# Loading the expert biases one attention unit sooner, into the room of the attention's operands

## The reference

```python
qk = jnp.einsum('bhdq,bhdl->bhql', qh, kh) * scale
sm = jax.nn.softmax(qk, axis=-1)
ret = jnp.einsum('bhql,bhdl->bhdq', sm, vh)
...
scores = xf @ gate_w.T + gate_b + bias
top_scores, top_idx = jax.lax.top_k(scores, TOP_K)
gates = jax.nn.softmax(top_scores, axis=-1)
comb = jnp.sum(jax.nn.one_hot(top_idx, E, dtype=gates.dtype) * gates[..., None], axis=1)
h = jax.nn.silu(jnp.einsum('td,ehd->teh', xf, w1) + b1)
y = jnp.einsum('teh,edh->ted', h, w2) + b2
out = jnp.einsum('ted,te->td', y, comb)
```

## Time and profile before

| what | us |
|---|---|
| median of 3 runs | 792.31 (791.72 to 800.5) |
| profiled execution, span | 789.6 |
| PE busy | 727.5 (92%) |
| DVE busy | 579.8 (73%) |
| ACT busy | 410.9 (52%) |
| POOL busy | 356.2 (45%) |

### The profile page before, as it was taken

The page is one execution under the profiler, slowest core; times in us unless marked ns, Lnnn a source line. Parts: engine busy times, 40 slices in busy tenths (PEclk is TensorE's granted clock), DMA queues, the critical chain, the costliest instruction groups (busy, mean ns, idle before and its releaser), DMA issues.

```text
span 789.6 us, 14359 instructions
## 1 busy us (share of the span) xinstructions
PE 727.5 (92%) x4237; PEld 305.2 (39%) x4265; DVE 579.8 (73%) x1148; ACT 410.9 (52%) x758; POOL 356.2 (45%) x347
## 2 busy tenths in 40 slices
PE   5989999899999999899999989989996889999992
PEld 2444444344444443222223222222233445555551
DVE  5688889795867778688988888998866775555551
ACT  2543445563636465377787767766783732222220
POOL 4665455113020131536657657767564723443332
PEclk9999999999999999899999999999998899999997
DMA  9999770017273678234343334544446677999963
GB/s 311 384 110 238 264 298 0 1 38 274 83 257 137 211 250 293 52 91 110 95 105 92 107 109 130 153 120 123 122 130 177 170 104 122 150 148 131 131 80 51
DMA packets 114326, 117.51 MB, mean 149 GB/s; under 512 B 54856, under 2 KB 78280, under 8 KB 114128
## 3 DMA queue, kind: packets, MB, share of 16 engines
q1 hardware_dynamic: 103152, 94.48, 42.1%
q0 software_dynamic: 10384, 22.02, 16.7%
q10 hardware_dynamic: 720, 0.13, 0.1%
HBM read 43.61 MB, written 59.56 MB: 131 GB/s over the span
## 4 chain that ended last, share of the span: by engine, by line
PE 43%; DVE 7%; issue 3%; SPq 1%; ACT 1%; DMA 1%; DVEq 1%; POOL 0%; POOLq 0%; ACTq 0%
PE l_b L1504 8%; PE l_a L1128 7%; PE l_pv L1515 7%; PE l_sm L1523 7%; PE l_pv L1149 4%; PE l_sm L1149 4%; PE l_a L1449 2%; PE l_b L1462 2%; DVE l_negm L1723 1%; PE l_a L1138 1%; PE l_b L1495 1%; DMA t_room<-in_b 1%; DVE h_negm L1723 1%; SPq L1073 1%; PE l_b L1456 1%
## 5 line engine op out<-in xcount | busy, mean ns | idle before, releaser
L1633 ACT ACTIVATE t_room<-l_b 128x512 f32<-128x512 f32 x256 | 139.1, 594 | 39.7 <-PE l_b L1504 38.9
L1128 PE MATMUL l_a<-w1h,h_stack 128*128 x312 | 78.9, 321 | 5.5 <-DVE l_stack L1181 3.9
L1723 DVE TENSOR_REDUCE l_negm<-l_a 128x2 f32<-128x1024 f32 x64 | 75.2, 1220 | 11.4 <-PE l_a L1449 11.4
L1723 DVE TENSOR_REDUCE h_negm<-l_a 128x2 f32<-128x1024 f32 x56 | 65.9, 1220 | 14.2 <-PE l_a L1449 14.2
L1157 ACT ACTIVATE l_stack<-l_stack 128x352 f32<-128x352 f32 x39 | 19.4, 496 | 106.3 <-DVE l_stack L1181 106.3
L1515 PE MATMUL l_pv<-t_room,l_vt 128*32 128x512 f32 x512 | 70.1, 620 | 0.1
L1523 PE MATMUL l_sm<-t_room,ones_f 128*32 128x512 f32 x512 | 69.5, 615 | 0.0
L825 PE MATMUL ps_st<-f_xt,wg 128*128 128x512 fp8e4 x256 | 65.7, 379 | 0.8 <-ACT f_xt L729 0.8
L825 PE MATMUL ps_r<-f_xt,wg 128*128 128x512 fp8e4 x256 | 65.7, 379 | 0.0
L974 POOL TENSOR_TENSOR X<-X,f_y 128x512 f32<-128x512 f32 x16 | 20.0, 1249 | 79.9 <-ACT f_y L875 79.9
L1128 PE MATMUL l_a<-w1l,h_stack 128*128 x156 | 50.2, 322 | 0.0
(11 more groups left out here) (301 smaller groups left out, 1572.6 us busy)
## 6 DMA issues: line engine op xcount, KB each, us to landing
slots_x<-empty SPq DMA_DIRECT2D x8, 2376.0 KB, 11.2
slots_x<-empty SPq DMA_DIRECT2D x7, 2112.0 KB, 16.3
h_stack<-h_parts SPq DMA_DIRECT2D x96, 64.0 KB
l_stack<-l_parts SPq DMA_DIRECT2D x96, 64.0 KB
f_stage<-in_w SPq DMA_DIRECT2D x8, 704.0 KB, 7.3
f_stage<-in_w SPq DMA_DIRECT2D x8, 512.0 KB
h_kf<-in_ctx SPq DMA_DIRECT2D x16, 256.0 KB, 3.2
l_vt<-in_ctx_t SPq DMA_DIRECT2D x16, 256.0 KB, 3.1
```

The costliest lines, as they stand in the source:

```text
L1128: mm = pe.matmul(self.HP[i % 2][:, 0:self.H], T.xt[i % T.AHEAD][:, xp * self.FC + f, :], self.w1[wp][:, bass.ds(e, 1), f * self.H:(f + 1) ...
L1633: act.activation(weights_at(u, c, h)[:, :], B[t % 2][:, :], ACT.Exp, scale=SCALE).then_inc(b_ok, 1)
L1723: dve.tensor_reduce(negm[u % 2][:, 2 * half:2 * half + 2, j], A[half][:, :, :], AX.X, ALU.max, negate=True)\
```

## The change

Four things. First, the second operand buffer (`parts1`), the first (`parts`) and the float rooms kf and qf are now parts of one tensor, `F.wide`, with 6 x 512 words. Its second part also serves as the buffer `xb` of layer 0's feed-forward network, which had one of its own. Second, b1 goes to the first 2816 words of `F.wide` rather than to `T.room`, in one transfer, issued at unit 15 of SyncE's loop, after the stacks are filled and the last `a_quad` has read the parts. Third, what lay over the parts moves to `T.room`: `ht` and one low part to its first 2 x 512 words (so that VectorE waits for the row sums `TC * NU - 1` before it sets their edges), the tables `passed` and `skipped` behind them, and four of the weighted outputs to the second half. Fourth, `normalise(15)` moves up, from behind `choose(3)` to in front of it.

```diff
@@ class FirstUnit
-        self.parts = sb("parts", [P, 4, D], BF16)
-        self.kf, self.qf = sb("kf", [P, D]), sb("qf", [P, D])
+        self.wide = sb("wide", [P, 6 * D])
+        parts = [self.wide[:, 2 * k * D:2 * (k + 1) * D].bitcast(BF16).rearrange("p (n d) -> p n d", d=D) for k in range(2)]
+        self.parts, self.parts1 = parts
+        self.kf, self.qf = self.wide[:, 4 * D:5 * D], self.wide[:, 5 * D:6 * D]
@@ class GroupOperands
-        self.xb = sb("xb", [P, G, D], BF16)
+        self.xb = xb
@@ class FirstTiles
-        self.b1s = self.room[:, 0:E * H].rearrange("p (e h) -> p e h", e=E)
+        self.b1s = F.wide[:, 0:E * H].rearrange("p (e h) -> p e h", e=E)
@@ bias
-            dve.wait_ge(self.T.b1_in, 32)
+            dve.wait_ge(self.T.b1_in, 16)
@@ head_attention
-        passed, skipped = (T.room[:, (H + k * TILES) * E:(H + (k + 1) * TILES) * E].rearrange("p (t e) -> p t e", e=E) for k in range(2))
+        passed, skipped = (T.room[:, 2 * D + k * TILES * E:2 * D + (k + 1) * TILES * E].rearrange("p (t e) -> p t e", e=E) for k in range(2))
...
-            "hl": [last_stack[:, at + 2 * HW:at + 3 * HW], last_parts[:, 0:HW]],
-            "ht": [four(last_parts[:, (1 + 2 * k) * HW:(3 + 2 * k) * HW]) for k in range(2)],
-            "y": [first_parts[:, 0:D], first_parts[:, D:2 * D], kf, qf, pvs[0], pvs[1], sums, r0],
+            "hl": [last_stack[:, at + 2 * HW:at + 3 * HW], first_room[:, 0:HW]],
+            "ht": [four(first_room[:, (1 + 2 * k) * HW:(3 + 2 * k) * HW]) for k in range(2)],
+            "y": [T.room[:, (4 + k) * D:(5 + k) * D] for k in range(4)] + [pvs[0], pvs[1], sums, r0],
@@ sync, in the loop over units
+                if u == NU - 1:
+                    for k in range(2):
+                        sp.wait_ge(stack_ok[k], STACKED * (NU // 2))
+                    sp.wait_ge(a_ps, 2 * TC * NU)
+                    sp.dma_start(T.b1s[:, :, :], b1.to_broadcast([P, E * H]).rearrange("p (e h) -> p e h", e=E)).then_inc(T.b1_in, 16)
@@ sync, behind the loop
-            soon = 4 * D // H
-            b1_wide = b1.to_broadcast([P, E * H]).rearrange("p (e h) -> p e h", e=E)
-            sp.wait_ge(sum_ps, TC * NU - 1)
-            sp.dma_start(T.b1s[:, 0:soon, :], b1_wide[:, 0:soon, :]).then_inc(T.b1_in, 16)
-            sp.wait_ge(sum_ps, TC * NU)
-            sp.dma_start(T.b1s[:, soon:E, :], b1_wide[:, soon:E, :]).then_inc(T.b1_in, 16)
@@ vector
             dve.wait_ge(b_ps, done("scores", NU - 1, STEPS - 1))
+            dve.wait_ge(sum_ps, TC * NU - 1)
             tiles.edges(dve)
             dve.wait_ge(table_ok, 1)
             tiles.bias(dve, 0)
+            normalise(NU - 1)
             choose(3)
-            normalise(NU - 1)
             tiles.bias(dve, 1)
```

More of the change, by code:

```diff
@@ L663, with __init__ @@
     G = 4
-    def __init__(self, nc, st, banks, ident_b, neg_half, D, HC):
+    def __init__(self, nc, st, banks, xb, ident_b, neg_half, D, HC):
         G, FC = self.G, D // P
@@ L1286, in head_attention @@
         kf, qf = F.kf, F.qf
-        parts = [F.parts, sb("parts1", [P, 4, D], BF16)]
+        parts = [F.parts, F.parts1]
         kh, kl, qh, ql = ([p[:, n] for p in parts] for n in range(4))
@@ L1331, in head_attention @@
         last_stack = stack[1][:, :, :, :].rearrange("p a h d -> p (a h d)")
-        last_parts = parts[1][:, :, :].rearrange("p n d -> p (n d)")
+        first_room = T.room[:, 0:2 * D].bitcast(BF16)
         wide = last_stack.bitcast(F32)
-        first_parts = parts[0][:, :, :].rearrange("p n d -> p (n d)").bitcast(F32)
         at = 8 * H
@@ L2197, in program @@
         banks = Banks(nc, two, D)
-        ops = GroupOperands(nc, two, banks, ident_b, neg_half, D, HID // P)
+        ops = GroupOperands(nc, two, banks, F.parts1, ident_b, neg_half, D, HID // P)
         block = two.enter_context(nc.Block())
```

## The result

| what | us |
|---|---|
| changed kernel, median of 20 runs (785.99 to 795.45) | 790.16 |
| kernel before, median of 20 runs in the same rounds (789.72 to 800.5) | 793.97 |
| ratio of the two | 0.9949, 95% interval 0.993 to 0.9968 |
| profiled execution after, span | 787.2 |

The change is a small gain, 0.51% or 4.0 us (2.5 to 5.6). 786.8 us was forecast, with 784.8 to 789.8 as the range: the median lies 0.4 us above it. Forecast was a saving of 5.5 us from 792.31.

The account below looks back on a forecast made before the run. The late expert bias load was taken to bound the hand-over from attention to tiles. Savings of 4.6 + 1.5 - 0.1 - 0.5 = 5.5 us gave 784.1, plus 2.7 made 786.8 us, range 784.8 to 789.8.

Parts of the forecast that it names:

- The wait that bounds, and its removal: VectorE's first bias addition, idle 5.22 us for the expert bias load, would start at about 594.6, 4.9 us earlier.
- The load at no cost: On SyncE's queue, the bias load issued at about 570 lands at about 577.6, ahead of tile 0's transfer, costing nothing.
- The addition beside GpSimd: VectorE's first bias addition reads PSUM, so GpSimd's L2010 would not hold it; if held, a loss of about 0.5 us.
- low_parts 4.6 earlier, with two holds: End of low_parts on VectorE: 6.4 us earlier at best, 4.4 if two GpSimd instructions hold VectorE; 4.6 taken.
- The normalization: Moved up on VectorE: costs 0.68 us either way, runs 595.3 to 596.0, and spares L2014 its 0.73 us wait.
- The clock term, 1.5 us: Without the 3.40 us gap TensorE runs the fourth product at full clock: 1.5 us more saved, 0 as other bound.
- The meeting at 606.0: VectorE and TensorE's first output product meet at about 606.0, 6.0 us earlier than before.
- From 612 to 648 ... they shift as one: VectorE and ScalarE carry the chain there with the same instructions, so the whole stretch moves earlier together.
- the fourth case: Something that doesn't move soaks up the gain from 612 to 648: 0 to 3.5 us saved; steady stretch after 645; chance 0.14.
- the second case: TensorE's light stretch from 598.7 to 601.4 drops the clock: 3.5 to 5.0 us saved; clock below 0.8; chance 0.20.
- What is given back, 0.5 us, on the choice of the last batch: GpSimd's L2023 meets VectorE's choice for the last batch: 0.5 us charged, bounds 0 and 0.8.
- The base: Starting time for the saving: profiled span 789.6 us plus 2.7 us to reach the median of runs shown, 792.31.

Follow-up runs that it names:

- load_late: Changed kernel with the bias load issued where it was before, behind four tile loads in two parts: 792.64 us, ratio 0.9985 to the kernel before.
- norm_back: Changed kernel with the last normalization back behind the choice of batch 3: 788.61 us, ratio 0.9912 to the kernel before.
- clock_fill: Kernel before with the twelve matmuls of TensorE's second hidden product made twice: 793.35 us, ratio 1.0005 to the kernel before.
- add0_late: Changed kernel with GpSimd's first scatter to the output moved behind unit 13's scatters and unit 15's low rows: 790.46 us, ratio 0.9976 to the kernel before.
- add_first: Changed kernel with GpSimd's residual addition of unit 15 ahead of the low rows of unit 14: 789.1 us, ratio 0.9949 to the kernel before.

## Why the prediction came out as it did

- **The wait that bounds, and its removal: right.** The first addition follows the memsets with no idle time. 4.9 us was its term, 5.4 came against the first profile, and 4.6 to 5.6 over the pairs of unedited profiles (8.9 to 9.7 before, 4.1 to 4.3 after).
- **The load at no cost: right.** Issued at 570.99; tile 0's transposed load was issued at 582.17, 0.8 us later than before in an execution whose first product came 1.2 us later. load_late shows the rooms free within about 2 us.
- **The addition beside GpSimd: right.** It ran 595.31 to 595.79, under L2011 (594.87 to 596.32), in 0.48 us. Forecast by the PSUM row, and by the rule of the Trainium skill (SBUF — State Buffer, Who interferes with whom); this trace agrees.
- **low_parts 4.6 earlier, with two holds: right**, 4.6 against the first profile and 4.3 in the mean of three. The bound of 6.4 without holds was not reached by any order tried: 10.5 to 11.0 in all twelve profiles with the early load, whether TensorE's second product had ended at 6.9 or at 8.6.
- **The normalization: worth nothing that shows**, by norm_back. I had claimed little for it by itself, but let it free "L2014 from 0.73 us of waiting"; GpSimd's L2024 stands ahead of it and set the time.
- **The clock term, 1.5 us: seen and then not kept.** The window has 1.00 where 0.72 stood, and from low_parts to the output product before takes 4.5, 2.7 and 4.2 us, after 2.7 to 2.9. Its reason was wrong: I tied the slow fourth product to the gap of 3.40 us, and clock_fill, without the gap, has it at 3.46. The sentence that the 0.72 stood only behind the gap misread the window: the clock was back at 1.00 behind the third product and fell again within the fourth. Windows of the kernel before:

```profile
604.00:606.50 2.50, 1.38 (x15) 1.03 (x15) 2.40 (x9) 1.03 (x4) 0.93 (x1) 1.00 0.27 102
607.00:610.00 3.00, 2.78 (x10) 1.52 (x10) 2.42 (x14) 1.85 (x3) 1.34 (x2) 0.50 0.46 89
```

  And the slowness comes and goes: it is in two of the three profiles of before. In the changed kernel a slow stretch lies on the second product (0.83 in 590 to 600), where VectorE's work covers it. That activity releases the throttled clock, as the Trainium skill has it (TensorE: Matmul & The Clock Gate, Part 1), is seen in clock_fill at 599.9.
- **The meeting at 606.0: right** against the first profile: w0 stands 16.3 behind the first product, forecast 606.0 - 589.77 = 16.2. Over three profiles of each the lead at w0 is 5.2 us and not 6.0, because the output product of before came at 17.5 and 18.9 in the other two profiles instead of 20.1.
- **"From 612 to 648 ... they shift as one": this step failed.** Between w0 and w1 the lead fell from 5.2 to 3.9 us. That is the fourth case's place (the pause begins at 612), and its mechanism in kind: something that does not move with TensorE ends the wait. By the signs given, the clock of 598 to 608 (0.97) rules out the second case, and the start of TensorE's unbroken chain (642.97, 644.89 and 645.80 in three profiles, forecast 642.5) passes the 645 of the fourth only once. What ends the wait for w1 is not the landing of the scatters nor a held VectorE, but the pause: w1 starts 10.3 to 10.6 us behind the first scatter of GpSimd's run wherever the pause shows. That run starts behind VectorE's slots, so it moved with low_parts (4.3), not with TensorE (5.3). I could not see it, because the one profile I had shows 1.17 us there, put down to "issue", and I didn't ask what that was. That the pause is also what the end lost is not shown: without it the two kernels lie 3.7 us apart, and the lead at w7 is 3.6 us with it and without it.
- **What is given back, 0.5 us, on the choice of the last batch:** the low rows fell elsewhere (615.32, while VectorE stood in the pause). A loss came, but elsewhere. A further 0.9 us, between w1 and the end, is not explained: that stretch differs by 1.2 us among the three profiles of the changed kernel alone. The lead is still 3.7 us at the hidden product of tile 20 (101.2 and 97.5), so 0.7 of these lie behind it, in the steady stretch.
- **The base: the other failed term.** I added 2.7 us to a sum of one profile to meet a median of three runs. Twenty runs in the same rounds as the changed kernel put that median at 793.97, 1.7 us higher. With it the same saving would have read 788.5. The forecast missed by 3.4 us: 1.7 from the base, 1.7 from the saving (5.5 against 3.8 between the medians). Over all three comparisons the saving is 5.2 us, so the forecast of it is not refuted by the times; the profiles, with a lead of 3.0 at the last scatter, speak for less.

## What to carry to other kernels

A sum read from one profile inherits that execution's landings, clock and pauses: a wait of 7.18 us was 6.23 in the next, a product of 3.29 us was 1.96. Where several profiles can't be had, widen the range by how much such terms can vary, and the base by the spread of the runs. A lead won on one engine counts only up to the next place where another one, with a smaller lead, ends the wait: write down the lead of every engine at each meeting, GpSimd's scatters included. An effect found in a trace (here the pause) is worth what taking it away from both kernels saves in time, and no more. And a gap with no releaser in front of an instruction whose inputs are ready is a question to settle before the sum.

## What the runs showed of the hardware

While GpSimd issued six or seven indirect transfers with 0.3 us between them, ScalarE stood still for 2.9 to 4.7 us and VectorE for 2.2 to 4.1 us with their inputs ready by TensorE's records, and TensorE stuttered, in eleven of the twelve profiles with such a run; with the run broken after four or five, ScalarE waited 0.30 to 1.22 us. What links the engines there isn't shown, nor why VectorE stood until 25.1 in add0_late, 2.9 us behind the end of its run of six. Instructions of VectorE with two inputs in SBUF were held until GpSimd's ended in the rows shown (L1189 took 1.77 instead of 0.52 us), and moving either of them chose another victim in norm_back and add_first. TensorE's granted clock fell to 0.50 within a product (before, the fourth, whose matmuls start at 0.31 us each and go on at 0.50) or ahead of one (changed, the second, behind 2.32 us of idle time), and in executions of the same kernel at different places.
